# The first batch's weights in two transfers, and one chunk fewer split into high and low parts

## The chip, the cores and the metric

The kernel runs on one core of a Trainium2 chip. The metric is the device time of one execution in microseconds (us), as the median of several runs. The engines are TensorE (PE), VectorE (DVE), ScalarE (ACT), GpSimd (POOL) and SyncE (SP); SP issues nearly all transfers between the chip's memory (HBM) and the core's own memory.

## The reference

Four residual layers run one after the other on x, which has 8 batches of 128 tokens and 512 features. All is in fp32. The change is in layer 0, in which each batch has a weight matrix of its own, picked by an index:

```python
def _L0_cond_ref(x, adapter_ids, weight):
    w = weight[adapter_ids]                      # weight: (16, 512, 512)
    return jnp.einsum('bsi,boi->bso', x, w)
...
x = x + _L0_cond_ref(x, itok_B_0_15, L0_cond_weight)
x = x + _L1_cond_ref(x, itok_B_0_7, ...)         # shared weights, plus gated low-rank experts
x = x + _L2_cond_ref(x, ..., itok_B_0_4)         # shared weights, plus a low-rank part by batch
x = x + _L3_cond_ref(x, ..., itok_B_2_6, 0)      # gate, up and down products, each plus a low-rank part
```

## The kernel before

All four layers are written out by hand, with one instruction stream for each engine and semaphores between them. Layer 0 is a loop over the 8 batches on PE, ACT, DVE and SP. The 512 input features are four chunks of 128 (`C` is 4), one 128-row contraction each. A batch's product is a sum of four chunks in one PSUM bank, with the tokens as the stationary operand and 512 output features as the moving one.

A chunk is computed in one of two ways. Either it goes through PE as fp32 (line 1447), straight from the raw weights `w0_raw` and the raw tokens `x_f`. Or both sides are split into a high and a low part of the faster type fp32r (`w0_hl` for the weights, `xa` for the tokens): ACT copies the high part (`high`, line 613), DVE subtracts it from the raw value to get the low part (`low`, line 945), and PE runs three matmuls (lines 1454 to 1456: high by high, high by low, low by high). `w0_chunks(b)` says which chunks are split: 2 and 3 for batch 0, and 1 to 3 for every other batch. So batch 0 has two fp32 chunks and the others one.

The weights come in by SP's queue, line 477, in the pieces that `w0_pieces(b)` gives. Batches 0 and 1 are one transfer of 1 MB each, with a whole row of 8 KB for each partition. Later batches are three transfers: chunks 0 and 1 (half rows, 4 KB), chunk 2, chunk 3. They land in a ring of four raw buffers. A transfer raises its semaphore by 16, and `w0_landed(b, c)` gives the semaphore and the count that say that chunk `c` of batch `b` is there. Before batch 4's weights are issued (lines 474 and 475) SP waits until PE has used batch 0's raw chunks (`w0_raw_used`) and DVE has split its last one (`w0_lo`); `w0_splits(b, c)` counts the splits.

The order on each engine is that of the code. PE: 14 warm-up matmuls (line 1438), then for each batch the fp32 chunks, the split chunks, and ahead of chunk 2 four transposes of the batch before (`transpose_y0`, line 1412). ACT: for each batch the high part of the tokens (`x0_high`), the high parts of the weights, and ahead of the last of them the copy of the finished batch before out of PSUM (`copy_y0`, line 625). DVE: for each batch `x0_low`, the low parts of the weights, then `x1_add` (line 957, the residual sum of the batch before, from PE's transposes) and `x1_low`, the low part of layer 1's input. From batch 3 on PE also runs four small matmuls of layer 1 for each batch (`thin1`, line 1430).

Of the kernel before, what the change touches and what calls it, by code (L numbers as in the profile page):

```python
# [37 lines left out]
C = D // P  # L38
# [14 lines left out]
KC = C - 1  # L53
WARM_UP = 14
W0_RING = 3
RAW_RING = 4
# [7 lines left out]
def bass_four_residual_layers(nc, xT, ids0, ids1, ids2, ids3, w0, w1, aw1, b1, w2, a2, b2, bias2,  # L64
                              wgu, agu, sel, bgu, wd, ad, bd, out):
    ctx = ExitStack()
    with ctx:
# [132 lines left out]
        def sem(name):  # L200
            return ctx.enter_context(nc.semaphore(name))
# [3 lines left out]
        w0_in = [[sem(f"w0_in{i}_{k}") for k in range(KC)] for i in range(RAW_RING)]  # L205
# [51 lines left out]

        def w0_pieces(b):

            return ((0, C),) if b < 2 else ((0, 2), (2, 3), (3, C))  # L260

        def w0_landed(b, c):

            if b < 2:
                return w0_in[b][0], 16
            piece = max(c - 1, 0)
            return w0_in[b % RAW_RING][piece], 16 * (b // RAW_RING + (b % RAW_RING < 2 and piece == 0 or b % RAW_RING > 1))

        def w0_chunks(b):

            return range(1 if b else 2, C)

        def w0_splits(b, c):

            return KC * b - 1 + c if b else c - 1

        def number(l, h, o):
# [178 lines left out]
        def _(sp):  # L458
            def ids_of(src, last):

                _, ids = nc.values_load_multi_w_load_instructions(
                    src[0:1, 0:B], engines=[mybir.EngineType.SP], min_val=0, max_val=last,
                    skip_runtime_bounds_check_because="each id only forms the DRAM address of a transfer, "
                                                      "and the transfer checks that address itself")
                return ids
# [3 lines left out]
            for b in range(B):  # L469
                adapter = adapter0[b]  # L470
                if b >= 2:
                    sp.dma_start(x_f[:, b], xT[b]).then_inc(x_in[b], 16)
                if b >= RAW_RING:
                    sp.wait_ge(w0_raw_used, b - RAW_RING + 1)
                    sp.wait_ge(w0_lo, w0_splits(b - RAW_RING, C - 1))
                for k, (first, end) in enumerate(w0_pieces(b)):
                    sp.dma_start(w0_raw[b % RAW_RING][:, first:end],
                                 w0[adapter][:, first * D:end * D]).then_inc(w0_in[b % RAW_RING][k], 16)
                if b == RAW_RING - 1:
                    sp.dma_start(aw1_raw[:], aw1).then_inc(aw1_in, 16)  # L480
                    sp.dma_start(lang_i[:], ids1.partition_broadcast(P)).then_inc(lang_in, 16)
# [6 lines left out]

            sp.wait_ge(w0_raw_used, 5)
            sp.wait_ge(w0_lo, w0_splits(4, C - 1))  # L490
            sp.dma_start(w2_raw[:], w2).then_inc(w2_in, 16)
            for b in range(B):
# [117 lines left out]
        def _(act):  # L610
# [22 lines left out]
            def x0_high(b):  # L633
                act.wait_ge(x_in[b], 16)
                c = w0_chunks(b).start
                high(xa[:, 0, c:C, b * S:(b + 1) * S], x_f[:, b, c:C]).then_inc(x0_hi, 1)
# [4 lines left out]
            for b in range(B):  # L641
                x0_high(b)
                if b >= W0_RING:
                    act.wait_ge(l0_tm, b - W0_RING + 1)
                for c in w0_chunks(b):
                    if c == C - 1 and b > 0:
                        copy_y0(b - 1)
                    act.wait_ge(*w0_landed(b, c))
                    high(w0_hl[b % W0_RING][:, 0, c - 1], w0_raw[b % RAW_RING][:, c]).then_inc(w0_hi, 1)
                if b == 7:  # L650
                    split_hi("w1_0")
                    split_hi("w1_1")
                if b >= 2:
                    x1_high(b - 2)
# [287 lines left out]
        def _(dve):  # L942
# [49 lines left out]
            def x0_low(b):  # L992
                cols = slice(b * S, (b + 1) * S)
                dve.wait_ge(x0_hi, b + 1)
                c = w0_chunks(b).start
                low(xa[:, 1, c:C, cols], x_f[:, b, c:C], xa[:, 0, c:C, cols]).then_inc(x0_lo, 1)

            for b in range(B):
                x0_low(b)
                for c in w0_chunks(b):  # L1000
                    dve.wait_ge(w0_hi, w0_splits(b, c))
                    low(w0_hl[b % W0_RING][:, 1, c - 1], w0_raw[b % RAW_RING][:, c],
                        w0_hl[b % W0_RING][:, 0, c - 1]).then_inc(w0_lo, 1)
                if b == 7:
                    split_lo("w1_0")
                    split_lo("w1_1")
                if b >= 1:
                    x1_add(b - 1)
                if b >= 2:
                    x1_low(b - 2)  # L1010
                if b == 4:
                    bias_of_language()
                if b >= 5:
                    sum_ranks1(0, b - 5)
# [394 lines left out]
        def _(pe):  # L1409
# [6 lines left out]
            def transpose_y0(b):  # L1416
                pe.wait_ge(y0_copied, b + 1)
                if b >= 2:
                    pe.wait_ge(x1_sum, b - 1)
                transposes(bank[2 + b % 2], [y0[b % 2][:, c * P:(c + 1) * P] for c in range(C)]).then_inc(l0_tr, 1)  # L1420


            def thin1(h, j):
                b = HB * h + j
                pe.wait_ge(x1_sum, b + 1)
                if h == 1:
                    pe.wait_ge(x1_sum, B)
                    pe.wait_ge(hg_lo, 1)
                for c in range(C):
                    ins = pe.matmul(thin1_bank(h, j)[:, 0:TM1], x_f[:, b, c], aw1_raw[:, c],  # L1430
                                    start=(c == 0), stop=(c == C - 1))
                ins.then_inc(l1_tm, 1)
# [6 lines left out]
            for b in range(B):  # L1439
                cols = slice(b * S, (b + 1) * S)  # L1440
                raw, hl = w0_raw[b % RAW_RING], w0_hl[b % W0_RING]
                pe.wait_ge(x_in[b], 16)
                if b >= 2:
                    pe.wait_ge(y0_copied, b - 1)
                pe.wait_ge(*w0_landed(b, 0))
                for c in range(w0_chunks(b).start):
                    ins = pe.matmul(bank[b % 2][:], x_f[:, b, c], raw[:, c], start=(c == 0), stop=False)  # L1447
                ins.then_inc(w0_raw_used, 1)
                pe.wait_ge(x0_lo, b + 1)
                for c in w0_chunks(b):  # L1450
                    if c == 2 and b > 0:
                        transpose_y0(b - 1)
                    pe.wait_ge(w0_lo, w0_splits(b, c))
                    pe.matmul(bank[b % 2][:], xa[:, 0, c, cols], hl[:, 0, c - 1], start=False, stop=False)  # L1454
                    pe.matmul(bank[b % 2][:], xa[:, 0, c, cols], hl[:, 1, c - 1], start=False, stop=False)
                    ins = pe.matmul(bank[b % 2][:], xa[:, 1, c, cols], hl[:, 0, c - 1], start=False,
                                    stop=(c == C - 1))
                ins.then_inc(l0_tm, 1)

                if b == 3:  # L1460
                    pe.wait_ge(aw1_in, 16)
                if 3 <= b < 7:
                    thin1(0, b - 3)
# [420 lines left out]
```

## Time and profile before

| | |
|---|---|
| median of 3 runs | 289.83 us (289.58 to 290.42) |
| the profiled execution's own time | 289.61 us |
| its span, first to last instruction | 287.8 us |
| PE, DVE, ACT, POOL busy | 279.9, 222.1, 153.8, 45.7 us |
| instructions | 4504 |
| bytes moved | 33.28 MB, 13.94 MB of them in the first 40 us |
| granted TensorE clock | 1.00 in every stretch, which is the 2.4 GHz level |

The profile page has the busy time of each engine, the span in 40 slices and the chain of work that ended last. The trace behind it can be asked for one engine's instructions in order of time, for that chain piece by piece, and for busy shares and bandwidth in a stretch. Times inside the execution count from the first instruction. A fp32 matmul on PE leaves two records, so "x4" on line 1447 is two matmuls.

### The profile page before, as it was taken

How to read it: one execution, taken by the hardware profiler on the slowest of the kernel's cores; microseconds unless marked ns; L12 is line 12 of the kernel's file. 1: busy time of each engine (PE TensorE's matmuls, PEld its weight loads, DVE VectorE, ACT ScalarE, POOL GpSimd, SP SyncE). 2: the span in 40 equal slices, each digit the busy share in tenths (PEclk: the TensorE clock that was granted, in tenths of full speed). 3: DMA queues.
4: the chain of work that ended last, by engine and by line, in shares of the span. 5: the costliest groups of instructions: out<-in, count | busy, mean ns of one | idle time of the engine just before them, and what ended most of it. 6: DMA issues, size and time to landing. Idle time of an engine off the chain costs nothing.

```text
span 287.8 us, 4504 instructions
## 1 busy us (share of the span) xinstructions
PE 279.9 (97%) x1579; PEld 231.4 (80%) x1579; DVE 222.1 (77%) x341; ACT 153.8 (53%) x250; POOL 45.7 (16%) x67
## 2 busy tenths in 40 slices
PE   6899999999999999999999999999999999999994
PEld 6567878988888878888888888888888888888883
DVE  0698897894656999988777785785788999999531
ACT  2787672413425269766736646646667989420000
POOL 1000000000804503424244034134000000000000
PEclk9999999999999999999999999999999999999999
DMA  5999953008504040120260350420390400000243
GB/s 203 373 399 397 401 170 109 0 0 254 185 0 101 2 132 19 34 114 0 79 214 3 122 170 2 128 92 0 86 380 29 131 2 0 0 2 0 73 127 93
DMA packets 22519, 33.28 MB, mean 116 GB/s; under 512 B 2528, under 2 KB 15328, under 8 KB 22112
## 3 DMA queue, kind: packets, MB, share of 16 engines
q1 hardware_dynamic: 22208, 32.47, 33.6%
q10 hardware_dynamic: 288, 0.52, 0.6%
q8 instruction: 12, 0.20, 0.3%
q14 instruction: 11, 0.09, 0.1%
HBM read 30.89 MB, written 2.10 MB: 115 GB/s over the span
## 4 chain that ended last, share of the span: by engine, by line
PE 95%; DMA 2%; DVE 1%; SPq 1%; issue 0%
PE bank L1593 12%; PE bank L1594 12%; PE bank L1595 12%; PE bank L1470 6%; PE bank L1472 6%; PE bank L1471 6%; PE bank L1733 5%; PE bank L1735 4%; PE bank L1736 4%; PE bank L1575 4%; PE bank L1430 3%; PE bank L1447 2%; PE bank L1749 2%; PE bank L1750 2%; PE bank L1751 2%; PE bank L1454 2%
## 5 line engine op out<-in xcount | busy, mean ns | idle before, releaser
L613 ACT ACTIVATE part<-bank 128x512 f32<-128x512 f32 x48 | 28.3, 595 | 56.0 <-PE bank L1595 35.2
L1196 DVE TENSOR_TENSOR part<-bank,part 128x512 f32<-128x512 f32 x44 | 29.1, 682 | 2.0 <-PE bank L1575 1.9
L1121 DVE SCALAR_TENSOR_TENSOR bgu_st<-bgu_st,lo_rows,bgu_raw 128x512 fp32r<-128x512 f32 x22 | 17.3, 823 | 12.2 <-ACT bgu_st L613 12.2
L945 DVE TENSOR_TENSOR w_hl<-w_raw,w_hl 128x512 fp32r<-128x512 f32 x31 | 20.0, 686 | 5.7 <-ACT w_hl L613 5.7
L613 ACT ACTIVATE w_hl<-w_raw 128x512 fp32r<-128x512 f32 x31 | 18.5, 622 | 5.6 <-DMA w_raw<-in_w 5.5
L595 POOL TENSOR_TENSOR s_tmp<-wgu_raw 128x256 f32<-128x256 f32 x11 | 8.4, 759 | 80.8 <-DVE wc_up L945 39.0
L1593 PE MATMUL bank<-xb,wc_gate 128*128 128x512 f32 x48 | 18.9, 394 | 0.0
L1595 PE MATMUL bank<-xb,wc_gate 128*128 128x512 f32 x48 | 18.9, 394 | 0.0
L1594 PE MATMUL bank<-xb,wc_gate 128*128 128x512 f32 x48 | 18.8, 392 | 0.0
L1575 PEld LDWEIGHTS bank<-t_st,bgu_st 128*128 128x128 f32 x88 | 14.7, 188 | 2.8 <-DVE t_st L1186 0.3
L613 ACT ACTIVATE xb<-x_f 128x512 fp32r<-128x512 f32 x14 | 8.8, 626 | 13.5 <-DVE x_f L1066 9.4
L1203 DVE TENSOR_TENSOR act_f<-part,act_f 128x512 f32<-128x512 f32 x20 | 15.1, 775 | 1.0
L1575 PE MATMUL bank<-t_st,bgu_st 128*128 128x256 f32 x88 | 15.8, 284 | 0.0
L1593 PE MATMUL bank<-xb,wc_up 128*128 128x512 f32 x40 | 15.8, 395 | 0.0
L1594 PE MATMUL bank<-xb,wc_up 128*128 128x512 f32 x40 | 15.7, 392 | 0.0
L1595 PE MATMUL bank<-xb,wc_up 128*128 128x512 f32 x40 | 15.6, 390 | 0.0
L766 ACT ACTIVATE act_f<-part 128x512 f32<-128x512 f32 x22 | 13.6, 629 | 2.1 <-DVE part L1196 2.1
L1594 PE MATMUL bank<-xt,wc_gate 128*128 128x512 f32 x36 | 14.1, 393 | 0.0
L1595 PE MATMUL bank<-xt,wc_gate 128*128 128x512 f32 x36 | 14.1, 393 | 0.0
L1593 PE MATMUL bank<-xt,wc_gate 128*128 128x512 f32 x36 | 14.1, 391 | 0.0
L613 ACT ACTIVATE bgu_st<-bgu_raw 128x512 fp32r<-128x512 f32 x22 | 12.7, 621 | 2.3 <-DMA bgu_raw<-in_bgu 2.3
L613 ACT ACTIVATE xa<-x_f 128x512 fp32r<-128x512 f32 (+2 forms) x16 | 9.0, 566 | 8.5 <-DVE x_f L1064 8.0
(225 smaller groups left out, 783.8 us busy)
## 6 DMA issues: line engine op xcount, KB each, us to landing
wgu_raw<-in_wgu SPq DMA_DIRECT2D x11, 512.0 KB, 4.3
bgu_raw<-in_bgu SPq DMA_DIRECT2D x40, 128.0 KB, 2.7
w_raw<-in_w SPq DMA_DIRECT2D x16, 256.0 KB, 10.6
w_raw<-in_w SPq DMA_DIRECT2D x3, 1024.0 KB, 6.7
w_raw<-in_w SPq DMA_DIRECT2D x6, 512.0 KB, 10.2
wd_raw<-in_wd SPq DMA_DIRECT2D x4, 704.0 KB, 6.0
out<-x_f SPq DMA_DIRECT2D x8, 256.0 KB, 2.4
x_f<-in_xT SPq DMA_DIRECT2D x6, 256.0 KB, 10.0
```

What stands on the lines that cost most here:

```text
L613: return act.activation(dst, src, ACT.Copy)
L945: return dve.tensor_tensor(dst, src, hi.bitcast(F32), ALU.subtract)
L1121: return dve.scalar_tensor_tensor(out=st, in0=st.bitcast(F32), scalar=lo_rows16[:, 0:1], in1=raw, op0=ALU.mult, op1=ALU.add)
L1196: dve.tensor_tensor(dst[:], bank[4 * (n % 2) + b][:], dst[:], ALU.add).then_inc(c_added, 1)
L1203: dve.tensor_tensor(dst, part[1][C_PART[k]][:], dst, ALU.mult).then_inc(act_mul, 1)
L1470: pe.matmul(dst, w_hi, x[0][:, cols], start=start, stop=False)
L1471: pe.matmul(dst, w_hi, x[1][:, cols], start=False, stop=False)
L1472: return pe.matmul(dst, w_lo, x[0][:, cols], start=False, stop=stop)
L1575: ins = pe.matmul(dst[:, q * 2 * S:(q + 1) * 2 * S], bgu_views(n, i)[1][:, pair], t3_st[:, g, pair * 2 * S:(pair + 1) * 2 * S], start=Fals ...
L1593: pe.matmul(dst[:], hi, x[0][c], start=(start and c == 0), stop=False, skip_group_check=True)
L1594: pe.matmul(dst[:], hi, x[1][c], start=False, stop=False, skip_group_check=True)
L1595: ins = pe.matmul(dst[:], lo, x[0][c], start=False, stop=(stop and c == 1), skip_group_check=True)
```

## The change

Batch 0's weights come in two transfers of half rows (chunks 0 and 1, then 2 and 3). Three of its chunks go through PE as fp32, each after a wait for its own piece, and only chunk 3 is split. `w0_landed` is written anew, so that it counts the pieces of every batch that shares a raw buffer, and `w0_splits` counts one split fewer.

```diff
         def w0_pieces(b):
 
-            return ((0, C),) if b < 2 else ((0, 2), (2, 3), (3, C))
+            return ((0, 2), (2, C)) if b == 0 else ((0, C),) if b == 1 else ((0, 2), (2, 3), (3, C))
 
         def w0_landed(b, c):
 
-            if b < 2:
-                return w0_in[b][0], 16
-            piece = max(c - 1, 0)
-            return w0_in[b % RAW_RING][piece], 16 * (b // RAW_RING + (b % RAW_RING < 2 and piece == 0 or b % RAW_RING > 1))
+            ring = range(b % RAW_RING, b + 1, RAW_RING)
+            piece = [first <= c < end for first, end in w0_pieces(b)].index(True)
+            return w0_in[b % RAW_RING][piece], 16 * sum(len(w0_pieces(i)) > piece for i in ring)
 
         def w0_chunks(b):
 
-            return range(1 if b else 2, C)
+            return range(1 if b else 3, C)
 
         def w0_splits(b, c):
 
-            return KC * b - 1 + c if b else c - 1
-
+            return KC * b - 2 + c if b else c - 2
...
                 pe.wait_ge(x_in[b], 16)
                 if b >= 2:
                     pe.wait_ge(y0_copied, b - 1)
-                pe.wait_ge(*w0_landed(b, 0))
                 for c in range(w0_chunks(b).start):
+                    pe.wait_ge(*w0_landed(b, c))
                     ins = pe.matmul(bank[b % 2][:], x_f[:, b, c], raw[:, c], start=(c == 0), stop=False)
                 ins.then_inc(w0_raw_used, 1)
```

How this stands on the engines, in the order of issue. PE, from the first matmul of batch 0 to the first of batch 1, before (`w_raw_52` and `w_hl_56` are batch 0's raw and split weights, `w_raw_53` batch 1's):

```order
L1447 MATMUL bank<-w_raw_52,x_f 128x512 [waits w0_in0_0,x_in0]
L1447 MATMUL bank<-w_raw_52,x_f 128x512
L1454 MATMUL bank<-w_hl_56,xa 128x512 [waits w0_lo,x0_lo]
L1455 MATMUL bank<-w_hl_56,xa 128x512
L1456 MATMUL bank<-w_hl_56,xa 128x512
L1454 MATMUL bank<-w_hl_56,xa 128x512 [waits w0_lo]
L1455 MATMUL bank<-w_hl_56,xa 128x512
L1456 MATMUL bank<-w_hl_56,xa 128x512
L1447 MATMUL bank<-w_raw_53,x_f 128x512 [waits w0_in1_0,x_in1]
```

The same place of the changed kernel, whose lines have moved up by two:

```order
L1445 MATMUL bank<-w_raw_52,x_f 128x512 [waits w0_in0_0,x_in0]
L1445 MATMUL bank<-w_raw_52,x_f 128x512 [waits w0_in0_0]
L1445 MATMUL bank<-w_raw_52,x_f 128x512 [waits w0_in0_1]
L1452 MATMUL bank<-w_hl_56,xa 128x512 [waits w0_lo,x0_lo]
L1453 MATMUL bank<-w_hl_56,xa 128x512
L1454 MATMUL bank<-w_hl_56,xa 128x512
L1445 MATMUL bank<-w_raw_53,x_f 128x512 [waits w0_in1_0,x_in1]
```

One fp32 matmul, with a wait for the second piece, has taken the place of three split ones. SP's queue from the load of the indices to batch 2's first piece (`w_raw_54`), before:

```order
L461 TENSOR_LOAD in_ids
L477 ISA
L477 DMA w_raw_52<-in_w 128x2048
L477 ISA
L477 DMA w_raw_53<-in_w 128x2048
L472 DMA x_f<-in_xT 128x512
L477 ISA
L477 DMA w_raw_54<-in_w 128x1024
```

And in the changed kernel:

```order
L459 TENSOR_LOAD in_ids
L475 ISA
L475 DMA w_raw_52<-in_w 128x1024
L475 ISA
L475 DMA w_raw_52<-in_w 128x1024
L475 ISA
L475 DMA w_raw_53<-in_w 128x2048
L470 DMA x_f<-in_xT 128x512
L475 ISA
L475 DMA w_raw_54<-in_w 128x1024
```

Batch 0's transfer has become two, and every later transfer of SP stands one transfer further back.

## Rows read from the trace of the kernel before

**Rows 1.** The page: busy time of each engine, and the ending chain by engine.

```profile
PE 279.9 (97%) x1579; PEld 231.4 (80%) x1579; DVE 222.1 (77%) x341; ACT 153.8 (53%) x250; POOL 45.7 (16%) x67
...
PE 95%; DMA 2%; DVE 1%; SPq 1%; issue 0%
```

**Rows 2.** The chain in order of time, 0 to 24 us: start, length, what.

```profile
3.29 4.79 DMA w_raw<-in_w
8.09 0.14 issue
8.22 1.95 PE bank L1447 x4
10.17 0.23 PE bank L1454
...
11.55 0.86 PE bank L1447 x2
12.41 0.23 PE bank L1454
...
13.10 0.44 PE bank L1412 x4
...
16.47 0.45 PE bank L1412 x4
16.93 0.02 issue
16.95 0.69 DVE x_f L957
...
18.71 0.61 DVE w_hl L945
19.32 0.14 issue
19.45 0.47 PE bank L1454
19.92 0.23 PE bank L1455
```

**Rows 3.** ACT in order of time, 0 to 25 us: start, length, line, tiles, [idle before].

```profile
8.11 1.15 ACT L613 ACTIVATE w_hl<-w_raw 128x512 fp32r<-128x512 f32 x2 [4.28 <-DMA w_raw<-in_w]
...
10.65 1.15 ACT L613 ACTIVATE w_hl<-w_raw 128x512 fp32r<-128x512 f32 x2 [0.98 <-DMA w_raw<-in_w]
...
20.66 1.25 ACT L613 ACTIVATE w_hl<-w_raw 128x512 fp32r<-128x512 f32 x2 [0.27 <-DMA w_raw<-in_w]
```

**Rows 4.** DVE in order of time, 0 to 25 us.

```profile
8.77 1.29 DVE L945 TENSOR_TENSOR w_hl<-w_raw,w_hl 128x512 fp32r<-128x512 f32 x2 [4.48 <-ACT w_hl L613]
...
11.32 1.29 DVE L945 TENSOR_TENSOR w_hl<-w_raw,w_hl 128x512 fp32r<-128x512 f32 x2 [0.79 <-ACT w_hl L613]
...
16.11 0.69 DVE L945 TENSOR_TENSOR w_hl<-w_raw,w_hl 128x512 fp32r<-128x512 f32 x1 [0.17 <-ACT w_hl L613]
...
22.53 1.89 DVE L945 TENSOR_TENSOR w_hl<-w_raw,w_hl 128x512 fp32r<-128x512 f32 x3
```

**Rows 5.** SP's queue in order of time, 0 to 25 us.

```profile
9.61 0.49 SPq L472 DMA_DIRECT2D x_f<-in_xT  x1
10.35 1.51 SPq L477 DMA_DIRECT2D w_raw<-in_w  x3
```

**Rows 6.** Busy time by stretch: PE, PEld, DVE, ACT, POOL, PEclk, DMA share, GB/s.

```profile
6.30:8.20 1.90, 0.00 (x0) 0.01 (x1) 0.00 (x0) 0.09 (x1) 0.00 (x0) 1.00 1.03 427
8.20:10.20 2.00, 1.98 (x5) 1.04 (x6) 1.43 (x3) 1.47 (x3) 0.00 (x0) 1.00 0.97 403
10.70:12.00 1.30, 1.30 (x6) 0.75 (x4) 0.68 (x2) 1.30 (x3) 0.00 (x0) 1.00 1.02 309
12.00:13.00 1.00, 1.00 (x5) 0.70 (x5) 0.77 (x3) 1.00 (x3) 0.00 (x0) 1.00 0.93 285
...
15.00:17.00 2.00, 2.00 (x11) 1.33 (x10) 1.68 (x4) 2.00 (x5) 0.00 (x0) 1.00 1.02 402
```

## The prediction, made before the changed kernel ran

> **What bounds the kernel.** I read the page first: PE is busy for 97% of the span, and 95% of the chain that ended last is PE [rows 1]. So the time only moves if PE's work gets shorter or one of its few gaps closes. The change is confined to the first 11 us, so I went through the chain there piece by piece [rows 2]. It runs so: batch 0's weight transfer (3.29 to 8.08), PE on batch 0 (8.22 to 11.55) and then PE without a gap through batches 1 and 2 to 16.93, a short stretch of DVE (16.95 to 19.32), and PE again from 19.45. Then I read ACT and DVE over the same stretch, because PE's split matmuls of batch 1 need what they make. ACT sat idle until batch 1's transfer landed, at about 10.62, and began at 10.65; DVE followed at 11.32 [rows 3, 4]. The reader should see that two things stand close together at batch 1: PE's own backlog, and this second path of transfer, ACT and DVE, which PE's backlog just covers.
>
> **PE on batch 0.** The two whole-row transfers landed at 8.08 and 10.62 [rows 2, 3], so 1 MB took 2.54 us once the queue ran. Half of that is 1.27. The first half row should land at 8.08 - 1.27 = 6.81, and with the 0.14 us between landing and matmul [rows 2] PE starts at 6.95 instead of 8.22. Two fp32 matmuls took 1.95 us from a standstill [rows 2]: 8.90. The second piece is wanted then, and it should have landed at about 8.1, so the added wait costs nothing; what is queued behind it is only the rest of batch 0. If it landed as late as 8.76 it would still be in time. The third fp32 matmul costs 0.86 us (batch 1's, x2 [rows 2]): 9.76. The split of chunk 3 must be there: ACT starts on it at 8.1 instead of second in the row, DVE would have it at about 8.77 + 0.61 = 9.38, a margin of 0.2 us with the 0.14 to PE. Its three matmuls are 3 x 0.23 = 0.69: batch 0 ends at 10.45.
>
> Before, batch 0 was 1.95 + 6 x 0.23 = 3.33 us long and ended at 11.55. So the work got longer by 0.86 - 0.69 = 0.17 us, the start came 1.27 earlier, and PE is free 1.10 us earlier. ACT and DVE each lose one split (0.6 us), but both stood idle ahead of batch 1 [rows 3, 4], so that is worth nothing.
>
> **What of the 1.10 us is left at batch 1.** PE cannot start batch 1 before its weights land. They are behind batch 0's two pieces in the same queue. Half rows may move a little slower than whole ones. The low bound is no difference: 403 GB/s in 8.2 to 10.2, whole rows, against 402 in 15 to 17, a mix of half and quarter rows. The high bound is 402 against the 427 GB/s of 6.3 to 8.2 [rows 6]: 1.05 MB at these rates is 2.61 against 2.46 us, so 0.15. I take 0.05, nearer to the first because the two landings (2.54 us apart, 413 GB/s) lie between. Batch 1 lands at 10.67. PE starts its fp32 chunk 0.14 later at 10.81, 0.74 earlier than before, and needs 0.86 us plus a start from standstill (the 1.95 above is 0.23 more than 2 x 0.86): 11.90.
>
> Now the cover is gone. Chunk 1 of batch 1 needs DVE's low part. DVE's instruction began at 11.32 and lasts 0.61 [rows 4, 2], and it hangs on the landing by way of ACT: 11.93, or 11.98 with the 0.05. PE takes it 0.14 later at 12.12; its first matmul from a standstill is 0.47 and the next two 0.23 each, as at 19.45 [rows 2]: 13.05. Before, chunk 1 ended at 13.10. **So of 1.10 us at the end of batch 0, 0.74 is left at the start of batch 1, and 0.05 after its first split chunk.** The rest becomes two new gaps on PE, 0.36 us ahead of batch 1 and 0.22 us ahead of its first split chunk, each followed by a slower start.
>
> From there PE is full again and all follows 0.05 earlier: the transposes to 16.93, which release DVE's sum at 16.95, then DVE's run of four instructions, then PE at 19.45. DVE itself would be ready for that sum a little before it, at about 16.8 (its low part ahead of it began at 16.11 and lasts 0.69 [rows 4]), so it does not take the 0.05 away.
>
> **SP's queue.** Each issue takes about half a microsecond of SP, so all later ones come about 0.5 later. Batch 1 is issued at about 4.5 and its data are wanted at 8. Batch 4's weights were issued at 10.35, just behind a 9.61 issue that had no gate [rows 5]; now they come at some 10.7. They have long transfers queued ahead of them. ACT did wait 0.27 us for them at 20.66, but DVE took the result up only at 22.53 [rows 3, 4]. ACT's 0.6 us leave about 1.2 us of slack there, more than the whole shift. If that cover failed, the cost would be what is over 1.2.
>
> **The sum.** 289.61 - 1.27 (earlier start) + 0.17 (longer work) + 0.36 + 0.22 (the two new gaps) + 0.23 + 0.24 (two starts from a standstill) = 289.56 for the profiled execution. That one ran 0.22 below the median of the runs shown; 289.83 less 0.05 is 289.78. Between these two I give 289.7. About 0.3% (0.87 us) is what a measurement of this kernel can tell from no change, so this is no measurable change.
>
> **Rivals.** *The gain is kept.* If the smaller transfer makes the first bytes flow sooner, both landings come sooner by that much, and the path by ACT and DVE with them. For it: 4.79 us from issue to landing less 2.54 of moving leaves 2.25 us before and behind, of which some may grow with the size. Against it: nothing in the trace shows so small a first transfer. At the most PE's 0.74 us at the start of batch 1 is kept whole: 289.61 - 0.74 = 288.87, and 289.1 from the median.
>
> *The first piece does not land early.* If both pieces share the engines so that both end at about 8.08, PE starts as before and only the longer work is left: batch 0 ends at 11.72 and batch 1's fp32 chunk at 12.58, which is later than the 12.12 of ACT and DVE, so these hide nothing and everything comes 0.17 later: 289.8 to 290.0.
>
> *Half rows move badly at the start (slower).* In 10.7 to 13, where batch 2's half rows move, the queue ran at 309 and 285 GB/s [rows 6], and I do not know why. Were batch 0's 1 MB to move so, it would take 3.39 to 3.68 us instead of 2.54, and batch 1 would land 0.85 to 1.14 us late. From a lateness of 0.10 on (0.05 over what I took) every part of it is paid, through ACT and DVE. That is 0.75 to 1.04 us: 290.4 to 290.9. It passes the 0.87 us from a lateness of 0.97. Against it: the same kind of piece is in 15 to 17, at 402.
>
> *Each transfer pays its fixed part (slower).* The extreme of it is that the 2.25 us are paid again in front of the second piece; then batch 1 lands 2.25 late, and 2.15 of it is paid: 291.8 to 292.0. The rows are against this: batch 1's transfer landed 2.54 us after batch 0's, with 403 GB/s between, so a queued transfer paid no such part. The Trainium skill (DMA: Bandwidth & Descriptors, sections on the anatomy of one DMA and on bandwidth) gives about 2.0 us fixed for each DMA plus its bytes at 436 GB/s, and the rule to batch to 1 MiB or more, which speaks against this change. By that rule as a sum over DMAs the change would cost some 2 us; the trace does not agree that queued transfers add it.
>
> **Chances.** The forecast (the 1.10 us absorbed, -0.15 to +0.1) 0.66; the gain kept in part or whole 0.14; the first piece not early 0.10; half rows slow 0.08; fixed part paid again 0.02. Of the second nearly all is still within 0.87 us; I give 0.05 to faster. Of the slow half rows about half is over 0.87, so with the last one 0.06 for slower, and 0.89 for the same. The range is 289.0, the gain kept, to 290.5, the lower part of slow half rows, and takes in the spread of the runs (289.58 to 290.42).
>
> **What would show it.** In the changed profile: the transfer on the chain 3.5 us long and PE's first fp32 matmul at about 6.95; three of them in batch 0 (x6); ACT's batch 0 split once, near 8.1; ACT on batch 1 at 10.7, as before; PE idle for about 0.4 ahead of batch 1's fp32 chunk, and a wait for DVE's `w_hl` ahead of its first split chunk at about 12.1; DVE's sum of batch 1 at 16.9 and PE's restart at 19.4, each within 0.1 of before. The prediction is wrong if ACT on batch 1 starts well away from 10.65: the whole time follows it. It is also wrong if DVE's sum at 16.95 moves by more than 0.3 us with that landing where it was.

## The result: 0.14% slower

The changed kernel takes 290.24 us in the median (290.05 to 290.94, 22 runs) against 289.86 us (289.58 to 290.42, 22 runs). The ratio is 1.0014, with a 95% interval of 1.0008 to 1.0021. That is 0.38 us: less than the 0.87 us named as no change, but on the other side of zero from the forecast 0.05 us of gain, and clear of noise. A second measurement of the same kernel gave 1.0007 (0.9998 to 1.0015).

The profiled execution took 290.85 us, near the top of its runs. Its page, busy times and ending chain:

```profile
PE 281.6 (97%) x1578; PEld 231.4 (80%) x1578; DVE 221.6 (77%) x340; ACT 153.0 (53%) x249; POOL 45.7 (16%) x67
...
PE 93%; DMA 3%; DVE 1%; SPq 1%; issue 0%; ACT 0%
```

Against [rows 1], PE has two points of the chain fewer, DMA has one more, and ACT has come onto it. The chain in order of time, to be held against [rows 2]:

```profile
4.46 7.79 DMA w_raw<-in_w
12.26 0.02 issue
12.28 0.64 ACT w_hl L611
12.92 0.02 issue
12.94 0.70 DVE w_hl L943
13.64 0.14 issue
13.78 0.47 PE bank L1452
...
18.55 0.69 DVE x_f L955
...
20.92 0.14 issue
21.06 0.47 PE bank L1452
```

The chain now begins with batch 1's transfer, not batch 0's, and goes by way of ACT and DVE to batch 1's first split matmul: the second path of the prediction, but 1.6 us late. DVE's sum came at 16.95 before and comes at 18.55; PE's restart went from 19.45 to 21.06. ACT over the same stretch shows the two landings [rows 3]:

```profile
9.56 0.63 ACT L611 ACTIVATE w_hl<-w_raw 128x512 fp32r<-128x512 f32 x1 [5.96 <-DMA w_raw<-in_w]
...
12.28 1.15 ACT L611 ACTIVATE w_hl<-w_raw 128x512 fp32r<-128x512 f32 x2 [1.68 <-DMA w_raw<-in_w]
```

Batch 0's second piece was there at 9.56 (forecast 8.1), batch 1's weights at 12.28 (forecast 10.67, before 10.65). And by stretch, with GB/s last [rows 6]:

```profile
4.30:6.30 2.00, 2.00 (x15) 2.00 (x15) 0.00 (x0) 0.00 (x0) 0.00 (x0) 1.00 0.79 205
6.30:8.30 2.00, 1.29 (x6) 0.72 (x6) 0.00 (x0) 0.00 (x0) 0.00 (x0) 1.00 1.02 369
8.30:10.70 2.40, 2.21 (x5) 0.49 (x3) 0.48 (x1) 1.04 (x2) 0.00 (x0) 1.00 0.96 382
10.70:13.00 2.30, 1.55 (x6) 0.78 (x5) 0.74 (x3) 0.72 (x2) 0.00 (x0) 1.00 1.01 401
```

The same stretches of the kernel before:

```profile
4.30:6.30 2.00, 1.96 (x17) 1.76 (x16) 0.00 (x0) 0.00 (x0) 0.00 (x0) 1.00 0.78 270
6.30:8.30 2.00, 0.08 (x1) 0.11 (x2) 0.00 (x0) 0.19 (x1) 0.00 (x0) 1.00 1.04 434
8.30:10.70 2.40, 2.40 (x7) 1.32 (x8) 1.76 (x3) 1.42 (x4) 0.00 (x0) 1.00 0.98 401
10.70:13.00 2.30, 2.30 (x10) 1.45 (x9) 1.45 (x3) 2.30 (x5) 0.00 (x0) 1.00 0.98 298
```

The reader should see a slow stretch that has moved. Before, the queue ran at 434 GB/s and then slowly at 298 in 10.7 to 13, where batch 2's pieces moved and nobody waited. Now it runs slowly from the start, and at 401 where it was slow. The DMA engines were busy all the same (share 0.98 in 10.7 to 13 before): the rows took longer.

The rates alone do not give the whole lateness. Up to 10.7 us the changed kernel had moved some 0.30 MB less (2.07 against 2.37 MB from 4.3 on), which at 400 GB/s is 0.76 us, and batch 1 came 1.63 late. The trace's single packets have the rest: when batch 1's last row arrived, 0.43 MB of what stands behind it in the queue had moved already, against 0.08 MB before, and these 0.35 MB are another 0.88 us. So some of the core's 16 DMA engines ran ahead while others were still at batch 1, whose last row came at 11.87 and whose landing followed at 12.25. (The packets do not name their engine; that some ran ahead of others is inferred.)

One more thing does not fit. PE's restart is 1.61 us late, but the span grew by 1.1 (287.8 to 288.9). The 0.5 us came back at the very end. DVE's last sum in order of time, kernel before and changed kernel:

```profile
283.83 0.69 DVE L1313 TENSOR_TENSOR x_f<-bank,part 128x512 f32<-128x512 f32 x1 [2.27 <-PE bank L1759]
```

```profile
285.48 0.69 DVE L1311 TENSOR_TENSOR x_f<-bank,part 128x512 f32<-128x512 f32 x1 [2.27 <-PE bank L1757]
```

The queues (packets, MB, share) and the issues (us from issue to landing last) in 284.4 to 288.9 us, kernel before (in the changed kernel this stretch also takes in the end of the output transfer ahead, hence its 925 packets):

```profile
q1 hardware_dynamic: 528, 0.26, 20.2%
q14 instruction: 1, 0.01, 0.9%
...
out<-x_f SPq DMA_DIRECT2D x1, 256.0 KB, 2.9
```

And the changed kernel:

```profile
q1 hardware_dynamic: 925, 0.46, 33.9%
out<-x_f SPq DMA_DIRECT2D x1, 256.0 KB, 2.3
```

Before, one transfer of an instruction queue (q14) fell amid the last output transfer, which took 2.9 us; in the changed kernel none did, and it took 2.3. The load is not gone: the changed kernel's trace has it at 290.0 us, after the span's end. I had not looked at the tail at all.

### The profile page after: what moved, and what is told of

It is laid out like the page before. It is cut to its first block, busy times and chain, and to the rows that moved or that the text cites. A ratio compares the mean times of both kernels' runs of the same rounds, so it can differ in the third digit from the quotient of the medians.

```text
span 288.9 us, 4503 instructions
## 1 busy us (share of the span) xinstructions
PE 281.6 (97%) x1578; PEld 231.4 (80%) x1578; DVE 221.6 (77%) x340; ACT 153.0 (53%) x249; POOL 45.7 (16%) x67
## 4 chain that ended last, share of the span: by engine, by line
PE 93%; DMA 3%; DVE 1%; SPq 1%; issue 0%; ACT 0%
PE bank L1591 12%; PE bank L1592 12%; PE bank L1593 12%; PE bank L1468 6%; PE bank L1470 6%; PE bank L1469 6%; PE bank L1731 5%; PE bank L1733 4%; PE bank L1734 4%; PE bank L1573 4%; DMA w_raw<-in_w 3%; PE bank L1428 3%; PE bank L1747 2%; PE bank L1748 2%; PE bank L1749 2%; PE bank L1452 2%
## 5 line engine op out<-in xcount | busy, mean ns | idle before, releaser
L943 DVE TENSOR_TENSOR w_hl<-w_raw,w_hl 128x512 fp32r<-128x512 f32 x30 | 19.4, 684 | 8.3 <-ACT w_hl L611 8.3
L611 ACT ACTIVATE w_hl<-w_raw 128x512 fp32r<-128x512 f32 x30 | 17.8, 621 | 7.8 <-DMA w_raw<-in_w 7.8
```

What stands on the lines that cost most here:

```text
L611: return act.activation(dst, src, ACT.Copy)
L943: return dve.tensor_tensor(dst, src, hi.bitcast(F32), ALU.subtract)
```

## The experiments

Thirteen further kernels ran, and the kernel before and the changed one once more. All diffs are against the changed kernel unless the text says otherwise. This table has what their profiles show; "tail" is the span's end less the end of DVE's last sum. The last column is the ratio to runs of the kernel before on the same chip, with its interval; those runs' medians lay between 289.74 and 289.96.

| kernel | ACT on batch 1 | DVE's last sum | tail | median | ratio |
|---|---|---|---|---|---|
| before | 10.65 | 283.83 | 3.3 | 289.86 | |
| before again | 10.66 | 283.92 | 3.4 | 289.84 | |
| changed | 12.28 | 285.48 | 2.7 | 290.24 | 1.0014 (1.0008-1.0021) |
| changed again | 11.61 | 284.80 | 2.7 | 290.14 | 1.0007 (0.9998-1.0015) |
| e1 chunks only | 10.83 | 284.26 | 2.7 | 289.50 | 0.9987 (0.9978-0.9996) |
| e2 transfers only | 11.63 | 284.85 | 3.3 | 290.82 | 1.0038 (1.0025-1.0050) |
| e3 halves contiguous | 12.00 | 285.18 | 2.7 | 290.41 | 1.0021 (1.0009-1.0033) |
| e4 cut by partition | 13.02 | 288.14 | 2.8 | 293.93 | 1.0149 (1.0131-1.0168) |
| e5 one transfer, 4 KB rows | 10.73 | 284.14 | 2.8 | 289.57 | 0.9984 (0.9968-0.9999) |
| e6 later issues held | 11.68 | 285.05 | 2.8 | 290.33 | 1.0021 (1.0008-1.0034) |
| e9 batch 1 halved | 10.16, 11.43 | 284.14 | 2.8 | 289.50 | 0.9988 (0.9979-0.9997) |
| e10 batch 2 whole | 10.61 | 284.03 | 2.8 | 289.53 | 0.9984 (0.9974-0.9994) |
| t1 chunks only, DVE +1 | 11.02 | 284.19 | 3.5 | 290.07 | 1.0009 (1.0000-1.0018) |
| t2 chunks only, ACT +1 | 10.81 | 284.21 | 2.7 | 289.52 | 0.9988 (0.9978-0.9997) |
| t3 two low parts merged | 10.66 | 284.68 | 3.4 | 290.65 | 1.0030 (1.0020-1.0040) |
| t4 before, memset on POOL | 10.80 | 284.51 | 2.7 | 289.38 | 0.9981 (0.9972-0.9990) |
| t5 changed, DVE +1 | 11.61 | 284.77 | 3.2 | 290.60 | 1.0032 (1.0021-1.0043) |

### The two halves of the change by themselves

e1 keeps the three fp32 chunks and goes back to one transfer:

```diff
-            return ((0, 2), (2, C)) if b == 0 else ((0, C),) if b == 1 else ((0, 2), (2, 3), (3, C))
+            return ((0, C),) if b < 2 else ((0, 2), (2, 3), (3, C))
```

> The arithmetic alone: one whole-row transfer as before, three fp32 chunks in batch 0. Theory A (the transfers make the loss, the third fp32 chunk costs only its 0.17 us): the first weights land at 8.1 and batch 1's at 10.6 as before, batch 0 ends 0.17 us later at 11.7, and the time is 0.1 to 0.2 us above the kernel before. Rival B (the third fp32 chunk makes the loss): 0.35 to 0.45 us above, as much as the whole change, with the landings unmoved.

e2 keeps the two transfers and goes back to two fp32 chunks:

```diff
-            return range(1 if b else 3, C)
+            return range(1 if b else 2, C)
...
-            return KC * b - 2 + c if b else c - 2
+            return KC * b - 1 + c if b else c - 1
```

> The transfers alone: batch 0 in two half-row transfers, two fp32 chunks and two split ones as before. Theory A: batch 1's weights land late, 0.4 to 1.6 us after 10.6, and since PE waits for them by way of ACT and DVE the time is as far above the kernel before as the whole change is, 0.3 to 0.5 us, with or without the third fp32 chunk. Rival B: the landings of batch 1 stay within 0.1 us of 10.6 and the time is within 0.1 us of before.

The landings came as theory A has them: 10.83 with the chunks alone, 11.63 with the transfers alone. But neither time is the one expected. The chunks alone are not 0.1 to 0.2 us slower than before but faster, by 0.13%. The transfers alone lose 0.38%, more than the whole change. So the change is a sum of a gain and a loss, and the table shows where each sits: every kernel with two fp32 chunks has a tail of 3.3 or 3.4, and those with three have 2.7 or 2.8, except where a kernel was given another DVE instruction or had one taken away (t1, t5 and t4 below).

### Why the first weights land late

e3 lays each of batch 0's halves out as one contiguous block in HBM, from an added array `w0h`:

```diff
-                    sp.dma_start(w0_raw[b % RAW_RING][:, first:end],
-                                 w0[adapter][:, first * D:end * D]).then_inc(w0_in[b % RAW_RING][k], 16)
+                    src = w0h[adapter][k * P:(k + 1) * P] if b == 0 else w0[adapter][:, first * D:end * D]
+                    sp.dma_start(w0_raw[b % RAW_RING][:, first:end], src).then_inc(w0_in[b % RAW_RING][k], 16)
```

> The changed kernel, but batch 0's two halves are each one contiguous block in HBM (an added array, laid out by the host), so that a 4 KB row is followed by the next one instead of by a gap of 4 KB. Theory A1 (the 8 KB pitch of the half rows makes them slow): the 4 KB rows move in 0.16 us each as they do later in the kernel, batch 1 lands at 10.6 to 10.8, and the time is that of the forecast, 0.0 to 0.1 us below before. Theory A2 (that there are two transfers at the cold start, or their rows of 4 KB, makes them slow, whatever the pitch): batch 1 lands as late as in the changed kernel and the time is 0.3 to 0.5 us above before.

Batch 1 landed at 12.00: as late as in the changed kernel. The gap of 4 KB between half rows is not the cause of that. But e3's stretches are others:

```profile
4.30:6.30 2.00, 2.00 (x11) 2.00 (x11) 0.00 (x0) 0.00 (x0) 0.00 (x0) 1.00 0.92 311
6.30:8.30 2.00, 2.00 (x11) 1.52 (x11) 0.00 (x0) 0.00 (x0) 0.00 (x0) 1.00 1.14 285
8.30:10.70 2.40, 2.04 (x6) 0.46 (x4) 0.91 (x2) 1.04 (x2) 0.00 (x0) 1.00 0.82 329
10.70:13.00 2.30, 1.76 (x5) 0.69 (x5) 0.59 (x2) 1.00 (x2) 0.00 (x0) 1.00 0.99 374
```

It started at 311 GB/s, not 205, and was slow from 6.3 to 10.7 instead. So the slow start itself may hang on the gap; with this one look that stays open.

e4 cuts batch 0's transfer by partitions, with whole rows:

```diff
+                    rows, cols = (slice(0, P), slice(first, end)) if b else (slice(64 * k, 64 * k + 64), slice(0, C))
+                    sp.dma_start(w0_raw[b % RAW_RING][rows, cols],
+                                 w0[adapter][rows, cols.start * D:cols.stop * D]).then_inc(w0_in[b % RAW_RING][k], 16)
...
+                if b == 0:
+                    act.wait_ge(*w0_landed(0, 0))
...
+                if b == 0:
+                    pe.wait_ge(*w0_landed(0, C - 1))
```

> The changed kernel, but batch 0's two transfers are partitions 0 to 63 and 64 to 127 with whole rows of 8 KB; PE and ACT wait for both. Theory A1 (pitch of the half rows): nothing is slow, both have landed at 8.1 to 8.2, batch 1 at 10.6 to 10.7, and only the 0.17 us of the third fp32 chunk and up to 0.1 us of waiting are left: 0.1 to 0.3 us above before. Theory A2 in the form that a second transfer at the start costs by itself: batch 1 lands 0.4 us or more late and the time is 0.5 us or more above before. In the form that 4 KB rows are the cost, it is as A1 says here, and the contiguous halves tell the two apart.

It lost 1.5%, far more than any theory had, and so decides nothing between them. Its stretches:

```profile
6.30:8.30 2.00, 1.28 (x8) 1.08 (x7) 0.00 (x0) 0.00 (x0) 0.00 (x0) 1.00 1.06 229
8.30:10.70 2.40, 0.02 (x1) 0.05 (x1) 0.00 (x0) 0.02 (x1) 0.00 (x0) 0.97 0.93 239
10.70:13.00 2.30, 2.30 (x3) 1.13 (x4) 1.16 (x2) 1.02 (x2) 0.00 (x0) 0.50 0.99 401
13.00:15.00 2.00, 2.00 (x5) 0.76 (x4) 1.29 (x2) 1.15 (x2) 0.00 (x0) 0.76 1.02 395
```

A transfer into 64 partitions ran at 229 to 239 GB/s, about half of the 434 above. PE, which had nothing to do from its warm-up to 10.68 (0.02 us busy in 8.3 to 10.7), then got a granted clock of 0.50, the 1.2 GHz level, and started batch 0 at that rate: its three fp32 matmuls took 4.43 us, against 2.81 in e1. A start 2.46 us late (10.68 against 8.22), these 1.62 and the 0.17 of the third chunk are 4.25 of the 4.31 us by which DVE's last sum was late.

e5 has one transfer again, but of 4 KB rows, against e1 (`w0h` as in e3):

```diff
+                    if b == 0:
+                        src = w0h[adapter].rearrange("(k p) n -> p k n", p=P)
+                        dst = dst.rearrange("p (k c) d -> p k (c d)", k=2)
...
```

> Three fp32 chunks in batch 0, whose weights come in one transfer as before, but made of 4 KB rows (two for each partition, the halves contiguous in HBM). Theory A3 (rows of 4 KB are slow while the queue starts): batch 0 lands 0.5 us or more after 8.3, batch 1 at 11.2 or later, and the time is 0.4 us or more above the kernel with the chunks alone (289.5). Theory A4 (it is the second transfer at the start, not the row length): the landings are those of the chunks alone, 8.1 to 8.4 and 10.6 to 10.9, and so is the time, within 0.15 us.

```profile
8.20 0.63 ACT L614 ACTIVATE w_hl<-w_raw 128x512 fp32r<-128x512 f32 x1 [4.52 <-DMA w_raw<-in_w0h]
10.73 1.15 ACT L614 ACTIVATE w_hl<-w_raw 128x512 fp32r<-128x512 f32 x2 [1.48 <-DMA w_raw<-in_w]
```

ACT in order of time shows landings as before. The row length is not the cause either: the same bytes in the same 4 KB rows are on time as one transfer (e5) and late as two (e3). And the queue still slows at batch 2, the first in pieces: 342 GB/s in 10.7 to 13.

e6 holds SP back after batch 1's issue, so that no further issue falls into the first transfers:

```diff
                 adapter = adapter0[b]
+                if b == 2:
+                    sp.wait_ge(w0_in[0][0], 16)
```

> The changed kernel, but SP issues batch 2's tokens and all that follows only when batch 0's first piece has landed. Theory A5 (SP's next issues disturb the transfers already running): the first three weight transfers run undisturbed, batch 1 lands at 10.6 to 10.8, and the time is 0.4 us or more below the changed kernel. Otherwise (the slowness lies in the transfers themselves): batch 1 lands as late as in the changed kernel, 11.3 to 12.3, and the time is within 0.2 us of it.

Batch 1 landed at 11.68 all the same. SP's later issues are not the cause.

e9 moves the cut to batch 1, against e1:

```diff
-            return ((0, C),) if b < 2 else ((0, 2), (2, 3), (3, C))
+            return ((0, C),) if b == 0 else ((0, 2), (2, C)) if b == 1 else ((0, 2), (2, 3), (3, C))
```

> Three fp32 chunks; batch 0 in one transfer, and batch 1 in two of half rows. If the loss comes with any weight transfer cut in half in the first 11 us: batch 1's second half lands 0.4 us or more after 10.75, at 11.2 or later; its first half still lands by 10.0, so that ACT starts on batch 1 early. If only a cut of the very first transfer costs: the halves land at about 9.5 and 10.8. In both cases PE has batch 0 until 11.7 and the time is that of the chunks alone, 289.4 to 289.7, unless the second half lands after 12.3, where PE would wait for it.

```profile
10.16 0.63 ACT L611 ACTIVATE w_hl<-w_raw 128x512 fp32r<-128x512 f32 x1 [0.88 <-DMA w_raw<-in_w]
11.43 0.63 ACT L611 ACTIVATE w_hl<-w_raw 128x512 fp32r<-128x512 f32 x1 [0.63 <-DMA w_raw<-in_w]
```

ACT shows batch 1's halves at 10.16 (expected by 10.0) and 11.43, the second 0.6 us after the 10.83 of the whole transfer in e1. So it need not be the very first transfer. The time does not mind, since PE has batch 0 until 11.7.

e10 moves it the other way and brings batch 2 whole as well, against e1 (`b < 3` in place of `b < 2`):

> Three fp32 chunks; batches 0, 1 and also 2 in one transfer each, so that batch 3 is the first in pieces. If the slow stretch comes with the first batch that is cut, wherever it stands: 10.7 to 13 us, slow at 285 to 309 GB/s in the kernel before, now runs at 380 or more, and a slow stretch of 280 to 330 GB/s stands at 13.3 to 15. If it belongs to that time or to batch 2: 10.7 to 13 stays at 285 to 310. PE may wait for batch 2, whose weights now land whole, by up to 0.5 us.

Stretches of e9, then of e10:

```profile
6.30:8.30 2.00, 1.17 (x8) 0.98 (x7) 0.00 (x0) 0.06 (x1) 0.00 (x0) 1.00 0.99 377
8.30:10.70 2.40, 2.35 (x7) 1.18 (x7) 1.16 (x2) 1.52 (x3) 0.00 (x0) 1.00 0.92 313
10.70:13.00 2.30, 2.30 (x9) 1.39 (x8) 1.39 (x2) 1.67 (x5) 0.00 (x0) 1.00 1.02 407
```

```profile
8.30:10.70 2.40, 2.40 (x7) 1.14 (x7) 1.16 (x2) 0.94 (x3) 0.00 (x0) 1.00 0.99 406
10.70:13.00 2.30, 2.30 (x9) 1.44 (x8) 1.39 (x3) 2.30 (x5) 0.00 (x0) 1.00 1.07 452
13.00:15.00 2.00, 2.00 (x13) 1.65 (x12) 1.86 (x4) 1.44 (x3) 0.00 (x0) 1.00 1.01 354
15.00:17.00 2.00, 2.00 (x11) 1.33 (x10) 1.79 (x3) 1.87 (x4) 0.00 (x0) 1.00 0.96 346
```

The 452 came as expected. e10's 354 misses the 280 to 330 expected for 13.3 to 15, but only because the stretches cut its slow place in two. Laid over that place, and over the one of the kernel before, the rates are alike, 284 before and 290 in e10:

```profile
10.75:12.50 1.75, 1.75 (x8) 1.04 (x7) 1.18 (x2) 1.75 (x4) 0.00 (x0) 1.00 1.01 284
14.20:15.50 1.30, 1.30 (x6) 0.75 (x4) 1.30 (x4) 1.11 (x3) 0.00 (x0) 1.00 1.00 290
```

So a slow stretch goes with the first batch that comes in pieces, wherever that stands: batch 0 (changed kernel, 205 GB/s at the start), batch 1 (e9, 313 in 8.3 to 10.7), batch 2 (before), batch 3 (e10, where 10.7 to 13 now runs at 452). In e9 and in the kernel before, the next two stretches run at 402 or more. That is not all of it: the changed kernel has a second dip in 13 to 15, 341 GB/s (322 in its second look, 321 in e2, 354 in e6), and e10 ran at 353 in 17 to 19 (393 before); no run explains these. Of these four kernels only the changed one makes PE wait for the slow stretch.

The changed kernel once more:

> The changed kernel once more, for a second look at its landings. If the late landing of batch 1's weights is a property of the change, they land at 11.3 to 12.3 us again (10.6 before) and the time is 0.3 to 0.5 us above the kernel before. If the first profile was an accident, they land at 10.6 to 10.8.

It landed at 11.61 and took 290.14 us: 0.95 late against 10.66 of the kernel before, looked at again. Here 0.23 MB less had moved up to 10.7, and 0.22 MB of later transfers had passed batch 1's last row (0.08 in the kernel before), which together are some 0.9 us. So the first look's larger lateness is mostly the larger unevenness.

> The kernel before once more, for a second look at its trace. Expected: landings at 8.0 to 8.4 and 10.6 to 10.9 us, and in its last 3.3 us again a transfer of the instruction queue amid the last output transfer, which then takes 3.2 us from DVE's last sum to the end of the span. If that tail is chance, it takes 2.7 us this time.

Both of its landings and its tail (2.9 us for the output transfer, with the instruction queue's transfer in the same stretch) were those of the first look.

### The tail

t1 and t2 are e1 with one instruction more, the tokens' low part (DVE) or high part (ACT) of batch 0 in two halves. For t1:

```diff
+                if b == 0:
+                    low(xa[:, 1, C - 1, 0:64], x_f[:, 0, C - 1, 0:64], xa[:, 0, C - 1, 0:64])
+                    low(xa[:, 1, C - 1, 64:S], x_f[:, 0, C - 1, 64:S], xa[:, 0, C - 1, 64:S]).then_inc(x0_lo, 1)
+                    return
```

> The chunks alone (three fp32 chunks, one transfer, 289.5 us), with one DVE instruction more: the low part of batch 0's tokens in two halves, while DVE idles. It gives DVE back the number of instructions that the kernel before had. Theory D (the last load of DVE's instructions, which falls amid the last output transfer in the kernel before, comes later with one DVE instruction fewer): the load is back amid the output transfer, which lands 2.8 to 2.9 us after its issue instead of 2.3, and the time is 0.3 to 0.6 us above 289.5. Otherwise (another engine's load): 2.3 us and 289.4 to 289.7.

> The chunks alone, with one ACT instruction more, the high part of batch 0's tokens in two halves, while ACT idles; DVE and PE as in the chunks alone. Theory D (DVE's load of instructions): nothing changes, the output transfer takes 2.3 us and the time is 289.4 to 289.7. Rival (ACT's load): the output transfer takes 2.8 to 2.9 us again, and the time is 0.3 to 0.6 us above 289.5.

Queues and issues from DVE's last sum to the span's end, t1:

```profile
q14 instruction: 1, 0.01, 1.3%
out<-x_f SPq DMA_DIRECT2D x1, 256.0 KB, 3.1
```

And t2, up to the landing:

```profile
q1 hardware_dynamic: 528, 0.26, 35.0%
out<-x_f SPq DMA_DIRECT2D x1, 256.0 KB, 2.3
```

One idle DVE instruction brought the instruction queue's transfer back into the output and cost 0.57 us (290.07 against 289.50 of e1). One ACT instruction cost nothing (t2, 289.52 on the same chip as t1). That the q14 transfer is DVE's own load of code is inferred from this; the rows don't name its engine.

t3 was to take one DVE instruction from the kernel before, by merging the low parts of chunks 2 and 3:

```diff
+                if b == 0:
+                    dve.wait_ge(w0_hi, 2)
+                    low(w0_hl[0][:, 1, 1:KC], w0_raw[0][:, 2:C], w0_hl[0][:, 0, 1:KC]).then_inc(w0_lo, 2)
+                for c in w0_chunks(b) if b else ():
```

> The kernel before (two fp32 chunks, one transfer) with one DVE instruction fewer: the low parts of batch 0's two split chunks in one instruction. Theory D: the last output transfer takes 2.3 us instead of 2.9, and the time is 0.4 to 0.6 us below before, 289.2 to 289.45, which is also 0.1 to 0.2 below the chunks alone, since the third fp32 chunk's 0.17 us is saved. Otherwise: no gain, 289.7 to 290.0, with the output transfer at 2.9.

It missed on both counts. The trace has 4504 instructions as before, one subtraction fewer but another instruction in its place, so the tail stayed (3.0 us for the output), and the test was void. And DVE began only when both high parts were there, at 9.40 instead of 8.77; PE waited for it at 10.78, and all ended 0.85 us late.

t4 does it properly, against the kernel before: one memset moves to POOL.

```diff
+            pool.memset(lo_rows16[0:32], 0.0).then_inc(masks_ready, 1)
...
-            for q in range(4):
+            for q in range(1, 4):
...
-                dve.wait_ge(masks_ready, 1)
+                dve.wait_ge(masks_ready, 2)
```

> The kernel before (two fp32 chunks, one transfer), with one of DVE's four small memsets at the start moved to POOL, so that DVE has one instruction fewer in the trace (447 as in the changed kernel; merging two low parts had left 448). Theory D (the load of DVE's instructions at the tail): the last output transfer takes 2.3 us from its issue instead of 2.9, PE's times are those of before, and the time is 0.4 to 0.6 us below before, 289.2 to 289.5. Otherwise the transfer takes 2.9 us and the time is that of before, 289.7 to 290.0.

t5 is the changed kernel with t1's edit:

> The changed kernel, with one DVE instruction more while DVE idles (448 again). If the change hides a gain at the tail behind its loss at the start, taking the gain away shows the loss alone: the output transfer takes 2.8 to 3.1 us, and the time is 290.6 to 290.9, as with the transfers alone (290.82). If the tail is not part of the change's sum: 290.1 to 290.3 as the changed kernel.

Both came out as theory D has them. t4 takes 289.38 us, 0.19% below before and the fastest kernel of the study. Its output transfer took 2.3 us. (Its profiled execution, at 289.87 the slowest of its runs, had some 0.5 us more on PE from 149 us on, where PE stood idle for DVE's `bgu_st` and DVE for ACT's; why ACT was late is not explained.) t5 takes 290.60, 0.36 above the first measurement of the changed kernel and 0.46 above the second, with 2.8 us for the output. Over all seventeen traces the output takes 2.8 us or more exactly where DVE has 448 records, and 2.3 where it has 447; the counts of PE and ACT do not part them so (t4 has those of the kernel before, and the short tail).

## Why the prediction was wrong, step by step

- **What bounds, and the second path: right.** Batch 1's first split matmul hangs on transfer, ACT and DVE, with some 0.10 us of slack, and lateness is paid in full beyond that. In the second looks at both kernels batch 1 was 0.95 us late and DVE's last sum 0.88; in the first looks 1.63 and 1.65. (DVE's first low part of batch 1 also took 0.70 us in both changed profiles, not the 0.61 assumed.)
- **The third fp32 matmul, 0.86 us: right.** Three took 2.81 us from a standstill (e1), two 1.96.
- **The first piece at 6.81: off by some 0.45.** PE began at 7.43 and 7.40 instead of 6.95.
- **The second piece "at about 8.1", in time up to 8.76: wrong.** ACT had it at 9.56 and 9.02. PE waited for DVE's split of chunk 3, which began on PE at 11.06 and 10.52, and batch 0 ended at 12.00 and 11.45: 0.45 later and 0.16 earlier than before, instead of 1.10 earlier.
- **"Batch 1 lands at 10.67", from a delay of 0.05 (bounds 0 to 0.15): this is the step that failed.** Batch 1 was 1.63 us late in the first look and 0.95 in the second. I took the rates of half rows from 15 to 17 us, long after the first batch in pieces, and compared steady with steady. The row for a start in pieces was there, 309 and 285 GB/s at 10.7 to 13, and I had it as a rival ("half rows move badly at the start") at 0.08, with a price of 0.75 to 1.04 us. That rival is what happened: at the price it named in the second look (0.88 at DVE's last sum), and beyond it in the first (1.65). Its name was wrong: e5 and e3 show that half rows are not the point, the cut into several transfers is. It also priced the rate alone, and not that the transfers behind get ahead of batch 1's last rows.
- **The fixed part paid again, 2.15 us: no.** DVE's last sum came 1.65 and 0.88 us late. The Trainium skill (DMA: Bandwidth & Descriptors, section "Anatomy of one DMA") has about 2.0 us fixed for each DMA, from a fit on transfers that GpSimd issues, while these are SP's; added up over DMAs that is an estimated 2 us more for the one more DMA. The traces do not agree: batch 1 landed 1.63 and 0.95 us late. The Trainium skill's rule to batch transfers to 1 MiB or more (same page, section "Bandwidth") did point the right way: one transfer of 1 MB did better than two halves (289.50 in e1, 290.24 in the changed kernel).
- **SP's later issues at no cost: right.** ACT waited 0.20 and 0.80 us for batch 4 in the two looks (0.27 before), and DVE did not wait for it in either.
- **Missing: the tail.** Taking one split from batch 0 leaves DVE one instruction fewer, and that moved a load of instructions out of the last output transfer, worth some 0.5 us (t1: 0.57, t4: 0.58, t5: 0.36 to 0.46 in the medians). I costed "ACT and DVE each lose one split" at nothing, which holds for their time and not for their count.

The sum with measured terms, changed again against before again: +0.88 at DVE's last sum, -0.7 at the tail, which is the 0.2 by which the span grew (288.0 to 288.2); the medians differ by 0.3 to 0.4. The range held the time only by luck: two missed terms, one of about a microsecond and one of half of one, stood against each other.

## What to carry over

Price a transfer by a stretch in the same situation, not by the steady rate: when a cut is moved to the front of a queue, look for what the trace shows where the first cut stands now, even if nobody waits there. Cutting the first load to start early pays only if its pieces, and what is queued behind them, still land in time; here whole transfers of 1 MB were better. Read the tail as well, and when an edit changes how many instructions an engine has, compare where its loads of code fall, above all against the last output.

## What was not expected of the hardware

- The first batch of weights in several transfers moved slowly wherever it stood: 284 GB/s over 1.75 us (before, batch 2), 290 over 1.3 us (e10, batch 3), 313 in 8.3 to 10.7 (e9, batch 1), against 401 to 452 in the same stretches where the cut stood elsewhere; at the very start it was 205 against 270. Why stays open: it is not the row length (e5), not later issues (e6), not the place in time (e9, e10), and the lateness is not the gap between rows (e3).
- Transfers in one queue do not end neatly one after the other: in the changed kernel 0.43 MB of later transfers had moved before the last row of batch 1 was there, against 0.08 MB before.
- Transfers of 512 KB into 64 partitions ran at 229 to 239 GB/s, about half the rate of one into 128 (e4). No run tells why.
- One load of instructions (0.01 MB) amid the last output transfer made it land in 2.8 to 3.1 us instead of 2.3. The kernel that avoids it (t4) is the version to keep: the old transfers, the old chunks, and one memset moved to POOL.
